# A convolution with mixed weight sets: the first images' operands in two row parts, weight points on TensorE, and statistics two tiles later

## The chip, the cores and the metric

The kernel runs on one core of one Trainium2 chip. The metric is the device time of one execution in microseconds. Every time below comes from the measured runs or from one profiled execution of the kernel before.

## The reference

`x` is 8 images of 64 channels and 48 x 48 pixels, float32. The reference normalizes each image over pairs of channels (32 groups), computes 8 logits for each pixel with a 1 x 1 convolution and takes their softmax, convolves the normalized image with 8 sets of 3 x 3 kernels to 64 channels each, adds a bias, and adds to `x` the sum of the 8 results weighted by the softmax:

```python
sel = jax.nn.softmax(conv1x1(gn(x), coupler_w) + coupler_b, axis=1)
sel = sel / sel.sum(axis=1, keepdims=True)
conv = conv3x3(gn(x), w).reshape(8, 8, 64, 48, 48) + bias
out = x + jnp.einsum('bschw,bshw->bchw', conv, sel)
```

## The kernel before

**Work and tiles.** Two images (64 channels each, so 128 partitions) make a round; there are four rounds. An image is 48 rows of 24 pairs of pixels, 1152 pairs, which are nine tiles of 128 pairs; a round has 18 tiles, nine of each image. A tile's results, two pixels by 512 columns (8 sets by 64 channels), lie in a `pair` of PSUM banks; three pairs are used in turn.

**The convolution.** Along a row it is computed from four "points": combinations of neighbouring pixels (`v_pts`, points 0 to 3), multiplied by matching combinations of the three kernel columns: point 0 half the sum of all three, point 1 the same with the middle one subtracted, points 2 and 3 an outer column itself. Each number is split in two float16 parts, a head and a tail. ScalarE makes the heads of `x` (`v_head`) and of the weights (`w_head`); tails (`v_tail`, `w_tail`) are the scaled value less the head, made by VectorE in the start and, for `x` in the rounds, by GpSimd (`input_tails`). SyncE's queue copies heads and tails into the operand layouts `op` and `op_two` (`fill_ops`, four transfers for each image and group of two points); a matmul takes 128 x 128 of them as weights and streams 512 columns of `w_head` or `w_tail`. `first_points` (points 0 and 1, nine matmuls) and `last_points` (points 2 and 3, ten) make 19 matmuls a tile.

**Order in a round.** TensorE's program does the last points of tile i, then the first points of tile i+2. ScalarE copies the first result, VectorE adds and subtracts (`seed`), so that the last points can be added on. Then VectorE multiplies the tile by the softmax weights (`multiply`: L640, L641), adds halves (`halve`: L649), and GpSimd adds quarters, what is left and the input (`finish`), with `input_and_bias` for three tiles at a time ahead of tiles 0 to 5. The pair of banks of tile i is free for tile i+3 when its half is done; the softmax weights of the next round are copied to `sel_now` at the round's end.

Between the tiles stand, in every engine's program by tile number, the steps of the next round: statistics (VectorE, tiles 0 and 1; aggregated at 2), `group_sums` (TensorE, 3), `group_variance` (VectorE, 4), `inverse_deviation` (GpSimd, 4), `scale_and_shift` (VectorE, 5), points (GpSimd, `POINTS_AT`), scaled points and heads (ScalarE, `HEADS_AT`, edges at `EDGES_AT`), tails (GpSimd, `TAILS_TILE`), `logits` (TensorE, 10), and the softmax (VectorE, 11 to 16).

**The start.** `x` comes in three loads, then the matrices for the group sums and six pieces of the weights (`w_low`, `w_high`: the two partition halves for each kernel row r). ScalarE takes the largest weight of each of three rows (`bound_of`, L506); VectorE and a tiny matmul turn it to a scale (`scales`), which every weight head needs. VectorE makes the weight sums and points (`kernel_sum`, `kernel_point1`, `kernel_point2`), point 0 and 3 of `x`, and all tails of `x` over the full 1152 pairs; GpSimd makes point 1 in three pieces and point 2 whole. TensorE does eight warm-up matmuls (L404), the logits of round 0, and waits for the operands:

```python
pe.wait_ge(ops_in[0][0], 16 * F_PARTS)
for a in range(2):
    for i in range(2):
        first_point(i, a, 0, i == 0)
first_points(2, 0)
```

## Time and profile before

| | us |
|---|---|
| median of 3 runs (352.16 to 352.71) | 352.54 |
| the profiled execution | 352.28 |
| its span, first to last instruction | 350.2 |
| TensorE busy | 314.3 |
| VectorE busy | 288.2 |
| GpSimd busy | 221.5 |
| ScalarE busy | 93.4 |

The engines overlap, so busy times don't add up. The page also shows the span in 40 slices, the transfers and the chain of waits that ended last.

### The profile page before, as it was taken

To read this page: it belongs to the slowest core of one execution; us is meant where nothing else is said; L and a number is where in the kernel's file an instruction comes from. 1 tells how busy PE (TensorE), PEld (TensorE's weight loads), DVE (VectorE), ACT (ScalarE), POOL (GpSimd) and SP (SyncE) were. 2 spreads that over 40 slices of the span, in tenths; PEclk is the share of its full clock that TensorE was granted. 3 is DMA by queue.
4 is the path that set the end of the run, shared out by engine and by line. 5 is a ranking of instruction groups with operands and counts; after the bars stand their busy time and mean duration, and the time that the engine had idled before them with its cause. 6 is when DMAs were issued, how large, how long until landed. Compare 5 with 4: busy or idle time off the path is not lost.

```text
span 350.2 us, 5352 instructions
## 1 busy us (share of the span) xinstructions
PE 314.3 (90%) x1612; PEld 142.9 (41%) x1612; DVE 288.2 (82%) x502; ACT 93.4 (27%) x127; POOL 221.5 (63%) x320
## 2 busy tenths in 40 slices
PE   0166779999999999999999999999999999999993
PEld 0142224444544434444544434445444344444441
DVE  2799999878799789877789699877789697777776
ACT  1665301162611201172521111173411111111110
POOL 3300068999793558999783568999774489533343
PEclk9996989999999999999999999999999999999998
DMA  6979996003984099005793198006770297002002
GB/s 194 212 147 195 306 198 139 4 0 97 214 195 116 6 254 219 5 0 154 155 239 70 47 240 196 0 0 176 160 147 1 79 236 172 0 3 66 0 0 67
DMA packets 28350, 41.24 MB, mean 118 GB/s; under 512 B 1968, under 2 KB 20528, under 8 KB 27952
## 3 DMA queue, kind: packets, MB, share of 16 engines
q1 hardware_dynamic: 27456, 37.49, 46.9%
q10 hardware_dynamic: 880, 3.58, 3.3%
q8 instruction: 6, 0.10, 0.1%
q14 instruction: 8, 0.07, 0.1%
HBM read 11.97 MB, written 4.72 MB: 48 GB/s over the span
## 4 chain that ended last, share of the span: by engine, by line
PE 66%; DVE 23%; issue 6%; DMA 2%; DVEq 1%; POOL 0%; SPq 0%; POOLq 0%
PE pair L342 41%; PE pair L354 14%; PE pair L350 10%; DVE high L641 4%; DVE pair L640 3%; DVE pair L624 3%; DVE pair L626 3%; DMA x_raw<-x 2%; DVE half L649 2%; DVE stats L544 1%; PE side L332 1%; DVE v_tail L800 1%; DVE w_tail L755 1%; DVE mix L609 1%; DVE w_sum L807 1%
## 5 line engine op out<-in xcount | busy, mean ns | idle before, releaser
L342 PE MATMUL pair<-w_head,op 128*128 128x512 f16 x864 | 236.4, 383 | 10.7 <-DVE half L649 5.5
L342 PEld LDWEIGHTS pair<-w_head,op 128*128 128x128 f16 x864 | 83.4, 99 | 116.6 <-DVE half L649 11.1
L354 PE MATMUL pair<-w_tail,op 128*128 128x512 f16 x288 | 109.9, 382 | 0.7 <-DVE w_tail L773 0.7
L479 ACT ACTIVATE m_sb<-pair 128x512 f32<-128x512 f32 x72 | 42.9, 597 | 225.9 <-PE pair L354 220.4
L937 POOL TENSOR_TENSOR quarter<-half 128x256 f32<-128x256 f32 x71 | 52.7, 743 | 72.4 <-DVE half L649 72.2
L640 DVE TENSOR_TENSOR pair<-pair,sel_now 128x512 f32<-128x512 f32 x71 | 49.5, 698 | 39.9 <-PE pair L354 39.4
L649 DVE TENSOR_TENSOR half<-pair,high 128x512 f32<-128x512 f32 x71 | 49.1, 692 | 9.9 <-DVE high L641 0.5
L350 PE MATMUL pair<-w_tail,op_two 128*128 128x512 f16 x144 | 54.6, 379 | 0.4 <-DVE w_tail L770 0.4
L624 DVE TENSOR_TENSOR pair<-pair,m_sb 128x512 f32<-128x512 f32 x72 | 49.6, 689 | 0.2
L626 DVE TENSOR_TENSOR pair<-m_sb,pair 128x512 f32<-128x512 f32 x72 | 49.3, 685 | 0.0
L641 DVE TENSOR_TENSOR high<-pair,sel_now 128x512 f32<-128x512 f32 x71 | 48.4, 681 | 0.0
L354 PEld LDWEIGHTS pair<-w_tail,op 128*128 128x128 f16 x288 | 28.3, 98 | 35.2 <-DVE w_tail L773 1.0
L925 POOL TENSOR_TENSOR bias_part<-bias_all,sel_now 128x384 f32<-128x384 f32 x24 | 19.9, 831 | 30.7 <-DVE sel_now L615 30.7
L941 POOL TENSOR_TENSOR mixed<-quarter 128x128 f32<-128x128 f32 x71 | 32.7, 461 | 5.6
L947 POOL TENSOR_TENSOR y_out<-mixed,x_res 128x128 f32<-128x128 f32 x71 | 32.4, 456 | 5.8 <-POOL mixed L941 0.5
L903 POOL TENSOR_TENSOR v_tail<-v_pts,v_head 128x576 f16<-128x576 f32 x24 | 30.2, 1281 | 0.0
L350 PE MATMUL pair<-w_tail,op 128*128 128x512 f16 x72 | 28.0, 389 | 0.5 <-DVE w_tail L755 0.5
L930 POOL TENSOR_TENSOR x_res<-x_res,bias_part 128x384 f32<-128x384 f32 x24 | 23.9, 997 | 2.3
L911 POOL TENSOR_TENSOR v_pts<-x_raw 128x1152 f32<-128x1152 f32 (+1 forms) x12 | 25.0, 2080 | 0.0
L350 PEld LDWEIGHTS pair<-w_tail,op_two 128*128 128x128 f16 x144 | 14.1, 98 | 17.7 <-DVE w_tail L770 0.9
L544 DVE BATCH_NORM_STATS2 stats<-x_raw 128x6 f32<-128x384 f32 x24 | 11.9, 548 | 5.9 <-DMA x_raw<-x 5.9
L450 ACT ACTIVATE v_head<-v_pts 128x1152 f16<-128x1152 f32 x12 | 14.0, 1165 | 0.7 <-ACT v_pts L441 0.4
(94 smaller groups left out, 148.2 us busy)
## 6 DMA issues: line engine op xcount, KB each, us to landing
op<-v_head SPq DMA_DIRECT2D x16, 600.0 KB, 7.8
op_two<-v_head SPq DMA_DIRECT2D x16, 300.0 KB, 9.0
op<-v_tail SPq DMA_DIRECT2D x16, 300.0 KB, 7.6
op<-v_head SPq DMA_DIRECT2D x16, 288.0 KB, 8.0
x_res<-x_pix SPq DMA_DIRECT2D x8, 576.0 KB, 6.9
out<-y_out SPq DMA_DIRECT2D x7, 576.0 KB, 3.9
x_raw<-x ACTq DMA_DIRECT2D x3, 1152.0 KB, 12.1
w_raw<-weight SPq DMA_DIRECT2D x6, 384.0 KB, 11.2
```

What stands on the lines that cost most here:

```text
L342: nc.tensor.matmul(dst, op[b][:, 0, j, at + r * PW:at + r * PW + P], w_head[:, j, r, :], start=fresh and r == 0, stop=False, skip_group_ch ...
L350: nc.tensor.matmul(dst, op[b][:, 0, j, after] if j == 0 else op_two[b][:, j - 2, after], w_tail[:, j, 1, :], start=False, stop=False, skip ...
L354: return nc.tensor.matmul(dst, op[b][:, 1, j, at:at + P], w_tail[:, j, 0, :], start=False, stop=True, skip_group_check=True)
L479: act.activation(m1_sb[:, i % LOOK, :], pair[i % SETS_OF_BANKS][:, 0, :], ACT.Copy) \
L624: dve.tensor_tensor(plus, minus, m1, ALU.add).then_inc(seeded, 1)
L626: dve.tensor_tensor(minus, m1, minus, ALU.subtract).then_inc(seeded, 1)
L640: dve.tensor_tensor(sets_of(i, 0), sets_of(i, 0), weights_of(i, 0), ALU.mult).then_inc(low_done, 1)
L641: dve.tensor_tensor(high[:, :, :, :], sets_of(i, SETS // 2), weights_of(i, SETS // 2), ALU.mult) \
L649: dve.tensor_tensor(half[:, i % LOOK, :, :, :].rearrange("p a s c -> p a (s c)"), pair[i % SETS_OF_BANKS][:, :, 0:N // 2], high[:, :, :, : ...
L937: pool.tensor_tensor(quarter[:, :, :, :].rearrange("p a s c -> p a (s c)"), hf[:, :, 0:2, :].rearrange("p a s c -> p a (s c)"), hf[:, :, 2 ...
L941: pool.tensor_tensor(mixed[:, :, :], quarter[:, :, 0, :], quarter[:, :, 1, :], ALU.add).then_inc(mixed_done, 1)
L947: pool.tensor_tensor(y_out[b][:, t, :, :], mixed[:, :, :], x_res[b][:, t, :, :], ALU.add).then_inc(out_done, 1)
```

## The change

Four edits are made together.

1. **Operands in two row parts.** For the first image pair, heads, tails and transfers of the operands are made first for rows 0 to 23 (`FIRST_ROWS`) and then for the rest. `first_fill(g, part)` issues five transfers in place of `fill_ops`' four. Parts run in the order (group 0, part 0), (1, 0), (0, 1), the load of `x_res`, (1, 1). TensorE waits for part 0 ahead of tiles 0 to 3, and for part 1 ahead of tile 4. The logits stand behind the first points of tiles 0 and 1.
2. **Weight points on TensorE.** `kernel_point1` adds the three kernel columns with float32 matmuls in a PSUM bank for each row r (a doubled identity as weights); `kernel_point2` subtracts twice the middle one in the same bank, once the point 1 head and tail are made. ScalarE and VectorE read heads and tails from there. The warm-up is 28 float32 matmuls of 128 columns ahead of the group sums, in place of eight float16 ones of 512 columns ahead of the logits.
3. **Three `x` points on GpSimd in pieces.** Points 1, 2 and 3 are made by GpSimd by thirds of the image; the last thirds of points 2 and 3 wait for the first weight head. GpSimd also makes the second part of the tails of points 2 and 3 (`late_tails`), after the first selection.
4. **Statistics two tiles later.** The statistics stand at tiles 2 and 3, aggregate 4, group sums 5, variance 6, scale 7; points at 5 to 8, heads 10 to 13, edges 11, tails 9 to 12, logits 11, the softmax from 12 on (divide_again and selection stay at 16). Round 0 of TensorE and all rounds of ScalarE are written out rather than looped.

```diff
+FIRST_ROWS = 24
+FIRST_PAIRS = FIRST_ROWS * PW
+FIRST_TILES = 4
...
-WARM = 8
+WARM = 28
...
-POINTS_AT = (5, 6, 8, 9)
-HEADS_AT = (8, 9, 12, 13)
-TAILS_TILE = (7, 8, 11, 12)
-EDGES_AT = 10
+POINTS_AT = (5, 6, 7, 8)
+HEADS_AT = (10, 11, 12, 13)
+TAILS_TILE = (9, 10, 11, 12)
+EDGES_AT = 11
...
+        w_points = [pair[2][:, 0, :], pair[2][:, 1, :], pair[1][:, 1, :]]
...
+            def first_fill(g, part):
+                pts = slice(2 * g, 2 * g + 2)
+                heads_made, tails_made, landed, fifth = ((h_first, t_first, first_in[g], first_in[g]),
+                                                         (h_done, t_done, ops_in[0][g], rest_in[g]))[part]
+                cols = slice(0, PW + FIRST_PAIRS) if part == 0 else slice(PW + FIRST_PAIRS, PADDED)
+                width = cols.stop - cols.start
+                below = slice(0, FIRST_PAIRS) if part == 0 else slice(FIRST_PAIRS, PAIRS)
+                above = slice(below.start + PW, below.stop + PW)
+                heads = v_head[0:C, pts, :]
+                wait(heads_made, 2 * g + 2)
+                sp.dma_start(op[0][0:C, 0, pts, cols], heads[:, :, cols]).then_inc(landed, 16)
+                sp.dma_start(op[0][0:C, 1, pts, cols], heads[:, :, cols]).then_inc(fifth, 16)
+                sp.dma_start(op[0][C:P, 1, pts, below], heads[:, :, above]).then_inc(landed, 16)
+                if g == 0:
+                    sp.dma_start(op_two[0][C:P, :, cols], v_head[0:C, 1, cols].unsqueeze(1).to_broadcast([C, 2, width])) \
+                        .then_inc(landed, 16)
+                else:
+                    sp.dma_start(op_two[0][0:C, :, cols], heads[:, :, cols]).then_inc(landed, 16)
+                wait(tails_made, 2 * g + 2)
+                sp.dma_start(op[0][C:P, 0, pts, cols], v_tail[0:C, pts, cols]).then_inc(landed, 16)
...
-            fill_ops(0, 0, 0)
-            fill_ops(0, 1, 0)
+            first_fill(0, 0)
+            first_fill(1, 0)
+            first_fill(0, 1)
             load_res(0, 0)
+            first_fill(1, 1)
...
-                    if more and i == 3:
+                    if more and i == 5:
                         group_sums(n + 1)
-                    if more and i == 10:
+                    if more and i == 11:
                         logits(n + 1)
...
+            def kernel_point1(r):
+                pe.wait_ge(w_low[r], 16)
+                for kx in range(K):
+                    last = nc.tensor.matmul(w_points[r], both_halves, w_raw[0:C, r, kx, :], start=kx == 0, stop=kx == K - 1)
+                last.then_inc(w_point1, 1)
+            def kernel_point2(r):
+                pe.wait_ge(w_high[r], 16)
+                pe.wait_ge(w_heads[0], r + 1)
+                pe.wait_ge(w_tails, r + 1)
+                nc.tensor.matmul(w_points[r], minus_twice, w_raw[C:P, r, 1, :], start=False, stop=True,
+                                 skip_group_check=True).then_inc(w_point2, 1)
+            pe.wait_ge(ready, 1)
+            for k in range(WARM):
+                nc.tensor.matmul(w_bank[:, 0:P], ones[:, :], ones[:, :], start=True, stop=True)
             pe.wait_ge(mats_loaded, 16)
             group_sums(0)
-            pe.wait_ge(ready, 1)
+            kernel_point1(0)
+            kernel_point1(1)
             pe.wait_ge(bounds_set, 2)
             pe.wait_ge(w_chain, 2)
             nc.tensor.matmul(w_bank[:, 0:2], ones[:, :], tiny[:, :], start=True, stop=False)
             nc.tensor.matmul(w_bank[:, 0:2], ones[:, :], w_max[:, :], start=False, stop=True).then_inc(w_added, 1)
+            kernel_point1(2)
+            for r in range(K):
+                kernel_point2(r)
+            pe.wait_ge(first_in[0], 16 * (F_PARTS + 1))
+            for i in range(2):
+                first_point(i, 0, 0, i == 0)
+            pe.wait_ge(c_tails, 1)
             pe.wait_ge(h_done, 1)
-            pe.wait_ge(w_chain, 3)
-            for k in range(WARM):
-                nc.tensor.matmul(w_bank[:, :], v_head[:, 1, 0:P], v_head[:, 1, 0:N], start=True, stop=True)
-            pe.wait_ge(c_tails, 1)
+            pe.wait_ge(h_first, 2)
+            pe.wait_ge(t_first, 2)
             logits(0)
-            pe.wait_ge(ops_in[0][0], 16 * F_PARTS)
-            for a in range(2):
-                for i in range(2):
-                    first_point(i, a, 0, i == 0)
+            first_point(0, 1, 0, True)
+            pe.wait_ge(w_tails, 6)
+            first_point(1, 1, 0)
             first_points(2, 0)
-            with pe.Fori(0, ROUNDS - 1) as n:
+            round_(0, True, True)
...
+            first_heads(1, 0)
             bound_of(1)
-            first_heads(1)
             bound_of(2)
-            first_heads(0)
+            first_heads(0, 0)
             act.wait_ge(w_chain, W_STEPS)
-            w_heads_of(0, slice(0, 1))
-            first_heads(2)
-            w_heads_of(0, slice(1, 2))
-            first_heads(3)
-            w_heads_of(0, slice(2, 3))
-            w_heads_of(1)
+            for r in range(K):
+                w_heads_row(0, r)
+            first_heads(1, 1)
+            first_heads(0, 1)
+            first_heads(2, 0)
+            first_heads(3, 0)
+            for r in range(K):
+                w_heads_row(1, r)
+            for r in range(K):
+                act.wait_ge(w_high[r], 16)
             w_heads_of(2)
+            copy_m1(0, 0)
+            w_heads_of(3)
             act.wait_ge(w_tails, 6)
             act.activation(w_tail[C:P, 3, 1, :], w_tail[C:P, 2, 1, :], ACT.Copy, scale=-1.0).then_inc(w_minus, 1)
-            w_heads_of(3)
+            exponentials(0)
+            copy_m1(1, 0)
+            first_heads(2, 1)
+            first_heads(3, 1)
             load_ahead(1)
...
-                    if more and i == 0:
+                    if more and i == 2:
                         dve.wait_ge(x_ahead, (n + 1) * 16)
                         statistics(range(CHUNKS // 2))
-                    if more and i == 1:
+                    if more and i == 3:
                         statistics(range(CHUNKS // 2, CHUNKS))
-                    if more and i == 2:
+                    if more and i == 4:
                         aggregate(n + 1)
-                    if more and i == 4:
+                    if more and i == 6:
                         group_variance(n + 1)
-                    if more and i == 5:
+                    if more and i == 7:
                         scale_and_shift(n + 1)
-                    if more and i == 11:
+                    if more and i == 12:
                         with_bias(n + 1)
                         maximum(n + 1)
-                    if more and i == 12:
+                    if more and i == 13:
                         less_maximum(n + 1)
-                    if more and i == 13:
+                    if more and i == 14:
...
             scale_and_shift(0)
-            first_input_point()
-            fourth_input_point()
-            input_tails_of(1, 1)
+            first_input_point(0)
+            input_tails_of(1, 0, 1)
+            first_input_point(1)
             weight_bound()
-            kernel_sum(0)
-            kernel_point1(0)
             scales()
-            input_tails_of(0, 2)
+            input_tails_of(0, 0, 2)
             coupler_parts()
-            kernel_sum(1)
-            kernel_point1(1)
-            input_tails_of(2, 3)
-            kernel_sum(2)
-            kernel_point1(2)
-            kernel_point2()
             first_point_tails()
-            input_tails_of(3, 4)
+            input_tails_of(1, 1, 1)
+            input_tails_of(0, 1, 2)
+            input_tails_of(2, 0, 3)
+            input_tails_of(3, 0, 4)
             second_point_tails()
...
-            for j in range(LOADS):
+            for j in range(LOADS - 1):
                 pool.wait_ge(x_loaded[j], 16)
-                raw_point(1, j)
+                for k in range(1, NP):
+                    raw_point(k, j)
+            pool.wait_ge(x_loaded[LOADS - 1], 16)
+            raw_point(1, LOADS - 1)
             inverse_deviation(0)
-            v_out, left, right = point_operands(2)
-            pool.tensor_tensor(v_out, left, right, ALU.subtract).then_inc(v_first[2], 1)
+            pool.wait_ge(w_heads[0], 1)
+            for k in range(2, NP):
+                raw_point(k, LOADS - 1)
+            def late_tails(k):
+                pool.wait_ge(h_done, k + 1)
+                pool.wait_ge(t_done, k)
+                cols = slice(PW + FIRST_PAIRS, PW + PAIRS)
+                pool.tensor_tensor(v_pts[:, k, FIRST_PAIRS:PAIRS], v_pts[:, k, FIRST_PAIRS:PAIRS],
+                                   norm_scale[:, 0:1].to_broadcast([P, PAIRS - FIRST_PAIRS]), ALU.mult).then_inc(late_scaled, 1)
+                pool.wait_ge(late_scaled, k - 1)
+                pool.tensor_tensor(v_tail[:, k, cols], v_pts[:, k, FIRST_PAIRS:PAIRS], v_head[:, k, cols],
+                                   ALU.subtract).then_inc(t_done, 1)
+            pool.wait_ge(sel_copied, 1)
+            for k in range(2, NP):
+                late_tails(k)
```

## Rows read from the trace of the kernel before

**Rows 1.** The page's first part: busy time of each engine, its share and instructions.

```profile
PE 314.3 (90%) x1612; PEld 142.9 (41%) x1612; DVE 288.2 (82%) x502; ACT 93.4 (27%) x127; POOL 221.5 (63%) x320
```

**Rows 2.** The chain of waits: start, duration in us, what.

```profile
88.79 1.34 PE side L332 x54
...
122.66 0.65 PE pair L342 x3
```

**Rows 3.** Timeline of TensorE: start, duration, operation, idle time before.

```profile
28.75 1.46 PE L342 MATMUL pair<-w_head,op 128*128 128x512 f16 x3 [3.47 <-DMA op<-v_tail]
...
47.77 1.46 PE L342 MATMUL pair<-w_head,op 128*128 128x512 f16 x3 [2.52 <-DVE half L649]
...
119.46 0.82 PE L342 MATMUL pair<-w_head,op 128*128 128x512 f16 x3 [0.62 <-DVE half L649]
...
137.09 0.28 PE L320 MATMUL side<-mean_var,mats 128*128 128x2 f32 x2
...
166.16 0.20 PE L332 MATMUL side<-cw_pts,v_head 128*128 128x32 f16 x2
```

**Rows 4.** Timeline of VectorE.

```profile
13.05 1.83 DVE L568 SCALAR_TENSOR_TENSOR shift<-group,norm_scale 128x1 f32<-128x1 f32 x1
...
20.06 0.15 DVE L828 TENSOR_SCALAR magnitude<-w_bank 128x2 int32<-128x2 int32 x1
...
22.72 0.69 DVE L807 TENSOR_TENSOR w_sum<-w_raw 128x512 f32<-128x512 f32 x1
...
28.38 2.31 DVE L755 SCALAR_TENSOR_TENSOR w_tail<-w_pts,half_scale,w_head 64x512 f16<-64x512 f32 x3
...
34.15 0.52 DVE L574 SCALAR_TENSOR_TENSOR logit<-side,undo,cb_all 128x288 f32<-128x288 f32 x1
...
45.60 0.70 DVE L640 TENSOR_TENSOR pair<-pair,sel_now 128x512 f32<-128x512 f32 x1 [0.25 <-DVE sel_now L615]
...
125.81 1.47 DVE L544 BATCH_NORM_STATS2 stats<-x_raw 128x6 f32<-128x384 f32 x3
...
160.31 0.70 DVE L640 TENSOR_TENSOR pair<-pair,sel_now 128x512 f32<-128x512 f32 x1 [0.79 <-PE pair L354]
...
161.74 0.69 DVE L649 TENSOR_TENSOR half<-pair,high 128x512 f32<-128x512 f32 x1
```

**Rows 5.** Windows: length, each engine's busy time, granted clock, DMA share, GB/s.

```profile
28.75:34.00 5.25, 4.71 (x11) 1.47 (x12) 5.15 (x7) 2.79 (x2) 0.00 (x0) 0.50 0.93 185
```

**Rows 6.** Timeline of ScalarE.

```profile
11.75 1.48 ACT L506 ACTIVATE w_pts<-w_raw 64x1536 f32<-64x1536 f32 x1 [6.75 <-DMA w_raw<-weight]
...
20.79 0.72 ACT L498 ACTIVATE w_head<-w_pts,half_scale 128x512 f16<-128x512 f32 x1 [1.82 <-DVE scale L835]
...
157.37 0.60 ACT L479 ACTIVATE m_sb<-pair 128x512 f32<-128x512 f32 x1 [0.66 <-PE pair L354]
```

**Rows 7.** Timeline of SyncE's queue, first operands.

```profile
19.05 0.68 SPq L252 DMA_DIRECT2D op<-v_head  x1
```

**Rows 8.** Timeline of GpSimd.

```profile
12.80 2.07 POOL L982 TENSOR_TENSOR v_pts<-x_raw 128x1104 f32<-128x1104 f32 x1
45.52 0.83 POOL L925 TENSOR_TENSOR bias_part<-bias_all,sel_now 128x384 f32<-128x384 f32 x1 [30.66 <-DVE sel_now L615]
46.43 0.99 POOL L930 TENSOR_TENSOR x_res<-x_res,bias_part 128x384 f32<-128x384 f32 x1
...
154.30 0.73 POOL L937 TENSOR_TENSOR quarter<-half 128x256 f32<-128x256 f32 x1
...
156.06 2.52 POOL L903 TENSOR_TENSOR v_tail<-v_pts,v_head 128x576 f16<-128x576 f32 x2
158.53 0.73 POOL L937 TENSOR_TENSOR quarter<-half 128x256 f32<-128x256 f32 x1
```

**Rows 9.** Groups of instructions, 6 to 45 us: busy, mean ns; idle before.

```profile
L404 PEld LDWEIGHTS w_bank<-v_head 128*128 128x128 f16 x8 | 1.0, 136 | 2.1 <-issue 2.1
...
L320 PEld LDWEIGHTS side<-mean_var,mats 128*128 128x128 f32 x2 | 0.5, 310 | 10.6 <-DMA mats<-matrices 10.6
```

More of the change, by code:

```diff
@@ L187, in program @@
         t_done = sem("t_done")
+        h_first = sem("h_first")
+        t_first = sem("t_first")
+        late_scaled = sem("late_scaled")
+        first_in = [sem(f"first_in{g}") for g in range(2)]
+        rest_in = [sem(f"rest_in{g}") for g in range(2)]
         logit_done = sem("logit_done")
@@ L324, in logits @@
             def logits(m):
+                pe.wait_ge(h_done, m * NP + 2)
                 pe.wait_ge(t_done, m * NP + 2)
@@ L339, in point @@
                 for r in range(K):
-                    if first and (j == 0 or r == 0):
+                    if first and (j < 2 or r == 0):
                         pe.wait_ge(w_heads[j], r + 1)
@@ L473, in load_ahead, with copy_m1, round_ @@
                 act.dma_start(x_raw[:, :], x_pair[m, :, :]).then_inc(x_ahead, 16)
[L475 removed]
+            def copy_m1(i, n):
+                act.wait_ge(m1_done, n * TILES + i + 1)
+                act.wait_ge(seeded, n * 2 * TILES + 2 * i + 2)
+                act.activation(m1_sb[:, i % LOOK, :], pair[i % SETS_OF_BANKS][:, 0, :], ACT.Copy).then_inc(m1_copied, 1)
+            def round_(n, more, ahead, copied=0):
                 for i in range(TILES):
[L477 to L480 removed]
+                    if i >= copied:
+                        copy_m1(i, n)
                     if more and i == EDGES_AT:
@@ L953, in round_ @@
                         finish(i, n)
-                    if more and i == 4:
+                    if more and i == 6:
                         inverse_deviation(n + 1)
@@ L1001 @@
     eye = np.eye(P, dtype=np.float32)
-    matrices = np.stack([0.5 * same_group, eye - 0.5 * same_group], axis=1)
+    matrices = np.stack([0.5 * same_group, eye - 0.5 * same_group, np.tile(eye[:C, :C], (2, 2)) * np.repeat([1, -2], C)[:, None]],
+                        axis=1).astype(np.float32)
     host = {
```

132 lines of the change are left out of this document (64 added, 68 removed).

## The prediction

> **What bounds the kernel now.** I read the page first: TensorE is busy nine tenths of the span [rows 1], so outside the start only its idle time can be won. The chain of waits then shows that a tile in the middle costs TensorE nothing but its own matmuls: 0.65 us for three of 512 columns, 0.216 us each, and 19 of them make 4.10 us a tile [rows 2]. VectorE needs less than that per tile, except where extra work is put between two tiles. The reader is to see two kinds of lost time.
>
> The first is the start. TensorE gets its first tile at 28.75 us, released by a transfer [rows 3], and VectorE multiplies the first tile only at 45.60 [rows 4]. In between, VectorE is one nearly unbroken queue: from the magnitude at 20.06 to the logits' bias at 34.15, then 11.45 us of softmax, weight tails and seeds to 45.60 [rows 4]. The DMA engines are busy at 0.93, 185 GB/s, while TensorE runs at a granted clock of 0.50, 1.2 GHz, having stood idle before 28.75 [rows 5, 3]. Tile 3 waits for the first half at 47.77, and its three matmuls take 1.46 us, the low level again, after 2.52 us of idleness [rows 3].
>
> The second is the head of each later round. From 119.46, where tile 2 begins, to the group sums at 137.09 there are 17.63 us [rows 3] for four tiles' work, 16.40 us: 1.23 us of idleness, because two lots of three statistics, 1.47 us, stand between VectorE's first tiles [rows 4]. About 0.2 us of it lies ahead of tile 3 and doesn't depend on them. Round 0 has no such loss: TensorE starts it late and slow.
>
> **The start after the change.** I walk the three engines in their new program orders; halves are 576 of 1152 columns.
>
> ScalarE: the first weight bound begins at 11.75 when its transfer lands [rows 6]. The third matrix adds 64 KB ahead of it, 0.35 us at 185 GB/s: 12.1. Three bounds (1.5 us each) with one half head between (0.7, as the 512-column head at 20.79) end at 17.4, the second half head at 18.1. Before, the first transfer of operands was issued at 19.05 [rows 7].
>
> VectorE no longer waits 1.83 us for the shift [rows 4]; this first shift isn't computed, its only user being a later round's point. Its queue is empty at 17.5 when the last bound comes. The bound sum is two tiny matmuls; I allow 0.8 us, so 18.3. The scales lie between 20.06 and ScalarE's first scaled head at 20.79: 0.7, so 19.0. Then one half tail (0.7; a weight tail of 512 columns is 0.77, a third of 2.31 [rows 4]), the coupler's small parts (I allow 0.7), three first-point weight tails 2.3, four more half tails 2.8, and three second-point weight tails 2.3. The seven operations that made weight sums and points (22.72 is one, 0.69) are gone: 19.0 + 8.8 = 27.8.
>
> Into this falls GpSimd's piecewise work: two last pieces of about 0.8 us each are held until the first weight head, so they start near 19.8, just where the coupler parts run. At 13.05 a one-column operation of VectorE lasted 1.83 us and ended at 14.88, when GpSimd's 2.07 us point from 12.80 ended at 14.87 [rows 4, 8]. So an operation with both inputs in SBUF can be held by one of GpSimd. I charge between 0 and 1.7 us and take 1.0: the logits' bias can start at 28.8. The Trainium skill's GPSIMD Engine Reference, section Key points, says that GpSimd shares its SBUF interfaces with VectorE and collides with instructions of two SBUF inputs; by that rule the sum keeps this 1.0, and without it the start would be 27.8; the trace agrees.
>
> TensorE: the nine float32 matmuls of the first point and three of the second have no row. One float32 matmul appears as two records; its weight load takes 310 ns against 136 ns for float16, both at low clock [rows 9]. The low bound is two float16 passes, 0.43 us; the high one 2 x 310/136 = 4.6 float16 prices at the low clock (0.427), 1.95 us. I take four prices at 2.4 GHz, 0.86, because the warm-up keeps TensorE busy until shortly before (the low end is float16's own work, the high end is the low clock, and a load isn't a stream). The Trainium skill's FP8 and Floating Point Precision, section TensorE Precision Notes, says that true FP32 makes four passes; by it a matmul would take 0.86 us or, at the low clock, 1.7, and no row here shows it. Rows 0 and 1 of point 1 then take 12.1 to 17.3, within the wait for the bound; row 2 takes 18.3 to 20.9. ScalarE turns them into heads at 0.65 each until 21.5, does four half heads and two edges (I allow 0.4 each) until 25.1, and the second point's rows until 27.0, each ahead of its VectorE tail. The second point's matmuls need the tails of point 1 at about 23.3 to 24.1, plus 0.86: no wait.
>
> The 28 warm-up matmuls of 128 columns cost 0.21 us each at 2.4 GHz, 0.43 at 1.2, from about 1.5 us. At the low clock for as long as after 28.75 (it was still 0.50 up to 34.00 [rows 5]) they end near 10, just ahead of the group sums, whose weight load waited until about 10.6 [rows 9]. I charge nothing; all at the low clock they would end at 13.5 and cost 2.9.
>
> The operands: a first part is 762 KB instead of 1488. Before, from the issue at 19.05 to the first tile it took 9.7 us [rows 7, 3]. The smaller one is issued at 18.2; half of that time and something for five separate issues gives 6.4: 24.6. Two first points (10 matmuls, 2.2) and the logits (1.34) [rows 2] end at 28.2, so VectorE's queue at 28.8 is the last to arrive; I take 29.0. From there the same operations as before take 11.45: first multiply at 40.45 instead of 45.60. Gain 5.15. The weights' last heads, the m1 copies (now moved ahead) and the other group's first part (due at 31, wanted at 33) are in time. The 2.5 us wait ahead of tile 3 and its slow matmuls move along unchanged.
>
> **What the start gives back.** The late tails are new on GpSimd, which before was idle until the selection at 45.52 [rows 8]; they wait for it too, at 40.3: two multiplies of 1.2 and two subtractions of 1.26 (half of the tail pair at 156.06), 4.9 us, so 45.2. Behind them stand the bias pair (45.52 to 47.42, 1.9 [rows 8]) and tile 0's finish at 47.1, while half 0 is ready at 42.5 (2.1 us from the multiply at 160.31 to the end of the half at 162.43 [rows 4]). SP's last operand transfer waits for the same tails, and behind it the second image's operands; these are wanted by tile 9, 20 us later, and cost nothing. GpSimd then has per tile a finish of 1.76 (154.30 to 156.06) and a bias pair, 3.6; a point is 2.06, a tail pair 2.5 [rows 8]. Tiles 0 to 4: 65.0; 5: 68.8; 6 with the deviation's 0.5: 73.1; 7: 76.9; 8: 80.7; 9 and 10 with tails: 84.9 and 89.2. TensorE reached the logits at 88.79 [rows 2]; it now wants them a tile of 4.10 later and 5.15 earlier: 87.7. Loss 1.5 in round 0.
>
> **The rounds.** Statistics two tiles later find a VectorE that waits 0.79 us of every tile [rows 4]. I walk it from F, the start of tile 2's first points: half 0 comes at F+6.35, and without statistics half 1 at F+9.6, a microsecond before TensorE wants it (F+10.6). Half 2 is ready at 12.8 (wanted 14.7), its seed behind the statistics at 15.4 (wanted 16.6); half 3 at 17.4 (wanted 18.8), its seed behind the second lot at 20.0 (wanted 20.7). So only the 0.2 ahead of tile 3 stays. Gain 1.0 in rounds 1 and 2, 2.0 in all; the bounds are nothing and the full 1.23 a round.
>
> But tails 1 moves from tile 8 to tile 10 and logits only from 10 to 11. In round 1 half 9 ends at 162.43 [rows 4]; GpSimd: finish 9 to 164.26, tails 0 to 166.75, finish 10 to 168.5, tails 1 to 171.0. The head of point 1 isn't later: tile 10's copy is at 157.37 [rows 6], and ScalarE's scale, head, copy, edges, scale and head (2.7, then to 161.5 for the next copy, then 0.6 + 0.7 + 2.4) bring it to 165.2. TensorE reached the logits at 166.16 [rows 3] and wants them at 170.3. Loss 0.8 in rounds 1 and 2. The softmax on VectorE begins one tile later and ends in the same tile. The round ended with 0.62 us of TensorE waiting for tile 17's half [rows 3]; one tile's slack of 0.79 less can add between nothing and 0.79 to it. I take the middle, 0.37, three times: 1.1.
>
> **Sum.** 5.15 + 2.0 - 1.5 - 1.6 - 1.1 = 2.95 us. The profiled execution took 352.28 us, 2.1 more than its span of 350.2 and 0.26 below the median of 352.54. So 349.3 for the execution, 349.6 for a median.
>
> **The rivals.** Within 0.2%, 0.7 us, a measurement can't tell a change here.
>
> First rival, no wait at the logits: GpSimd's order has room that I don't see, and the two later rounds and round 0 lose nothing there. For it, GpSimd kept up with the halves in this trace where no tails stood; against, a finish and a tail pair, 4.24, are longer than a tile. That is 3.1 us more gained: 346.5.
>
> Second, the operands land no sooner: they are rows of 1200 bytes and five issues, and if the count of pieces rather than the bytes sets their time, the first tile starts again 9.5 us after its issue, at 27.7 and the logits end 31.4; the bias follows at once. Gain 2.8 instead of 5.15: 352.0, no difference. A microsecond of slower issue more gives 353.0. For it, ten issues stand where eight did; against, the DMA engines are 0.93 busy, with bytes, in this stretch [rows 5]. I put it at 352.4.
>
> Third, on the other side: the float32 matmuls. Everything scales with their price d. Rows 0 and 1 must be through before the bound sum, and row 2 follows, nine in one line. At 1.2 us rows 0 and 1 end at 19.3, the bound sum at 20.1 and row 2 at 23.7, the chain is 2.8 us late, and nothing is left of the gain; at 1.7, the low clock throughout, the first bias comes at about 35.8, 6.8 late: 356.4, slower. The decisive point is 1.2 us. Against it, the clock came back under steady matmuls after 28.75 in this trace [rows 3, 5]: the matmuls of the middle run at 0.216.
>
> **How the numbers follow.** Forecast 0.60 (its own range 348.2 to 351.5, by a hold of 0 to 1.7, operands 1.5 us late, and waits at the logits from half to one and a half); no logits wait 0.14; operands no sooner 0.15; slow float32 matmuls 0.11. The range 347.2 to 352.8 takes in the second rival and part of the first, and leaves out about 0.18. Faster by over 0.2%: 0.60 + 0.14 = 0.74 and 0.01 from the partial cases of the others; same 0.14; slower 0.11.
>
> **What would show it.** Right: first tile near 24.6 at full clock, first bias near 29, first multiply near 40.5, waits of TensorE for v_tail ahead of the logits in three rounds (about 1.5, 0.8, 0.8), no idleness after tile 2 in rounds 1 and 2. Wrong: warm-up or w_points matmuls in front of the group or bound sums, w_points longer than 1.2 us each, first operands after 27, or VectorE held long beside GpSimd's pieces.

## The result and the profile after

The changed kernel takes 358.88 us, the median of 4 runs (358.80 to 359.66); the kernel before takes 352.62 beside it (352.16 to 352.71). The ratio is 1.0191, 95% interval 1.0178 to 1.0204: slower by 1.9%, outside the range and on the other side of no change. The profiled executions are 357.1 and 350.2 us long in their spans, 6.9 apart.

The page's first part, and the chain of waits from 10 to 40 us (start, duration, what):

```profile
PE 336.3 (94%) x1684; PEld 156.9 (44%) x1684; DVE 280.1 (78%) x496; ACT 93.7 (26%) x133; POOL 228.8 (64%) x329
```

```profile
2.61 9.92 DMA w_raw<-weight
12.53 0.04 issue
12.57 10.34 PE pair L435 x12
22.91 0.52 PE w_bank L455 x2
23.43 0.43 PE w_bank L456 x2
23.86 4.56 PE pair L435 x5
28.42 0.75 PE pair L443
29.16 0.11 PE pair L435
29.27 4.16 PE pair L443 x5
33.43 1.40 PE pair L374 x3
...
37.36 1.35 PE side L364 x54
38.72 0.03 issue
38.74 0.53 DVE logit L653
```

Behind the first weights' transfer, VectorE and DMA no longer stand in the chain of the start: from the landing at 12.57 to the logits' bias at 38.74 it is TensorE alone, whose busy time rose by 22.0 us over [rows 1]. A float32 matmul leaves two records, so twelve records of L435 are six matmuls and 10.34 us is 1.72 us for each; all twelve matmuls with the bound sum in their middle take from 12.57 to 33.4. The windows (columns as in [rows 5]) show the granted clock:

```profile
12.00:14.00 2.00, 1.43 (x2) 0.63 (x3) 1.25 (x5) 1.45 (x2) 0.55 (x1) 0.72 1.02 218
14.00:16.00 2.00, 2.00 (x4) 0.78 (x3) 1.21 (x3) 2.00 (x4) 0.00 (x0) 0.50 1.02 218
...
34.00:36.00 2.00, 2.00 (x6) 0.71 (x5) 1.97 (x4) 2.00 (x4) 0.00 (x0) 0.50 0.52 113
36.00:38.00 2.00, 2.00 (x37) 1.22 (x36) 0.51 (x1) 2.00 (x3) 0.00 (x0) 0.81 0.89 195
```

TensorE is busy in every window from 14 to 36, and the clock stays at 0.50, 1.2 GHz. It comes back only near 36.7, after 3.4 us of float16 matmuls. VectorE's timeline shows what it waits for:

```profile
17.96 0.15 DVE L887 TENSOR_REDUCE w_max<-w_max_part 64x1 f32<-64x3 f32 x1 [1.58 <-ACT w_junk L574]
23.89 0.16 DVE L892 TENSOR_SCALAR magnitude<-w_bank 128x2 int32<-128x2 int32 x1 [5.79 <-PE w_bank L456]
...
38.74 0.52 DVE L653 SCALAR_TENSOR_TENSOR logit<-side,undo,cb_all 128x288 f32<-128x288 f32 x1 [2.23 <-PE side L364]
...
50.12 0.70 DVE L719 TENSOR_TENSOR pair<-pair,sel_now 128x512 f32<-128x512 f32 x1 [0.25 <-DVE sel_now L694]
...
81.33 0.15 DVE L641 TENSOR_SCALAR norm_scale<-rstd 128x1 f32<-128x1 f32 x1 [1.75 <-POOL rstd L953]
81.52 1.77 DVE L647 SCALAR_TENSOR_TENSOR shift<-group,norm_scale 128x1 f32<-128x1 f32 x1
```

The bound is ready at 17.96, but its two tiny matmuls stand behind rows 0 and 1 on TensorE, 4.8 us. The first multiply, 45.60 before [rows 4], is at 50.12: 4.52 later. From there on TensorE's timeline, tile 3, then the waits of round 0, and the logits of round 1:

```profile
52.29 0.82 PE L374 MATMUL pair<-w_head,op 128*128 128x512 f16 x3 [2.53 <-DVE half L728]
...
84.05 0.81 PE L374 MATMUL pair<-w_head,op 128*128 128x512 f16 x3 [0.57 <-DVE pair L703]
...
86.57 0.82 PE L374 MATMUL pair<-w_head,op 128*128 128x512 f16 x3 [0.20 <-DVE half L728]
...
99.39 0.20 PE L364 MATMUL side<-cw_pts,v_head 128*128 128x32 f16 x2 [2.51 <-POOL v_tail L964]
...
126.27 0.82 PE L374 MATMUL pair<-w_head,op 128*128 128x512 f16 x3 [0.76 <-DVE half L728]
...
176.97 0.20 PE L364 MATMUL side<-cw_pts,v_head 128*128 128x32 f16 x2 [0.73 <-POOL v_tail L964]
```

I call the time from tile 3's first matmul to the next round's tile 2 the rest of round 0. It was 71.69 us, 47.77 to 119.46 [rows 3], and is 73.98, 52.29 to 126.27: TensorE is idle for 4.05 us of it and was for 0.62, and it is busy for 1.14 less, because before the clock was low at tile 3:

```profile
48.00:50.00 2.00, 2.00 (x6) 0.70 (x5) 2.00 (x5) 0.00 (x0) 1.75 (x4) 0.50 1.09 215
```

Rounds 1 and 2 take 77.58 each, before 77.53 and 77.54; the last one 75.67 in both. So 4.52 + 2.29 + 0.1 = 6.9: the start and the rest of round 0 hold the whole loss.

### The profile page after: what moved, and what is told of

It is laid out like the page before. It is cut to its first block, busy times and chain, and to the rows that moved or that the text cites. A ratio compares the mean times of both kernels' runs of the same rounds, so it can differ in the third digit from the quotient of the medians.

```text
span 357.1 us, 5439 instructions
## 1 busy us (share of the span) xinstructions
PE 336.3 (94%) x1684; PEld 156.9 (44%) x1684; DVE 280.1 (78%) x496; ACT 93.7 (26%) x133; POOL 228.8 (64%) x329
## 4 chain that ended last, share of the span: by engine, by line
PE 57%; DVE 16%; POOL 16%; issue 6%; DMA 3%; DVEq 1%; POOLq 0%; SPq 0%
PE pair L374 31%; PE pair L386 10%; PE pair L382 8%; POOL v_tail L964 4%; PE pair L435 4%; DVE high L720 3%; POOL quarter L998 3%; DVE pair L719 3%; DMA w_raw<-weight 3%; POOL v_pts L972 2%; DVE pair L703 2%; POOL mixed L1002 2%; DVE pair L705 2%; DVE half L728 2%; PE side L364 2%
## 5 line engine op out<-in xcount | busy, mean ns | idle before, releaser
L728 DVE TENSOR_TENSOR half<-pair,high 128x512 f32<-128x512 f32 x71 | 49.1, 692 | 9.8 <-DVE high L720 0.5
L977 POOL TENSOR_TENSOR v_pts<-x_raw 128x368 f32<-128x368 f32 (+1 forms) x9 | 7.0, 813 | 17.1 <-ACT w_head L567 12.5
L1054 POOL TENSOR_TENSOR v_pts<-v_pts,norm_scale 128x576 f32<-128x576 f32 x2 | 2.3, 1146 | 23.1 <-DVE sel_now L694 23.0
```

Of the source, the lines that this page charges most:

```text
L728: dve.tensor_tensor(half[:, i % LOOK, :, :, :].rearrange("p a s c -> p a (s c)"), pair[i % SETS_OF_BANKS][:, :, 0:N // 2], high[:, :, :, : ...
```

## The experiments

My theory of the start after this look: the twelve float32 matmuls are a line of 20.6 us on TensorE because they run at the low clock throughout, and they do so since they fill only 64 of 128 rows. The rivals: the clock hangs on the columns or the length of a matmul, or on the stage; or the line's place does the harm, ahead of the bound sum, and not its length. For round 0 it is GpSimd's late tails against the new order of the statistics. Unless it says otherwise, an experiment is the changed kernel with one edit. The price of a float32 matmul below is that of its two records together.

The clock blurs every comparison of round 0. In each trace but the changed kernel's it falls once or twice more after 42 us, to 0.50 for some three microseconds: near tile 3, and near the logits. Where TensorE has work then, this costs 1.2 to 1.6 us (the table at the end of this section gives its busy and idle time in the rest of round 0); where it would have waited anyway, nothing. At the logits it fell in six of the seven traces where TensorE had waited about 1.9 us or more for the tails, and in none of the six with a wait under 0.9. The changed kernel's trace is the seventh: it waited 2.51 us there and 2.53 ahead of tile 3, and the clock didn't fall. What decides on the fall near tile 3 no experiment here shows.

**Weight points on VectorE again**, the rest of the change left.

```diff
-            kernel_point1(0)
-            kernel_point1(1)
...
-            kernel_point1(2)
-            for r in range(K):
-                kernel_point2(r)
...
+                dve.tensor_tensor(w_sum[:, r, :], w_raw[:, r, 0, :], w_raw[:, r, 2, :], ALU.add).then_inc(w_sums, 1)
...
+                dve.tensor_tensor(w_pts[:, 0, r, :], w_sum[:, r, :], w_raw[:, r, 1, :], ALU.add).then_inc(w_point1, 1)
...
+                dve.tensor_tensor(w_pts[:, 1, :, :], w_sum[:, :, :], w_raw[:, :, 1, :], ALU.subtract).then_inc(w_point2, 1)
```

> The changed kernel with both weight points made by VectorE in SBUF again, everything else as changed. Theory A (the twelve float32 matmuls in one line on TensorE, 20.6 us of them, are what made the start late): the logits' bias on VectorE moves from 38.7 us to between 34 and 36, the first multiply from 50.1 to between 45.5 and 47.5, and the time falls from 358.9 by 3 to 4.5 us, to 354.4 to 356. What is left over 352.6 is then round 0, which lost about 4 us to GpSimd's late tails (2.3 net of the clock it kept). Rival (the row parts, their ten issues and the held pieces made the start late): the bias stays near 38 and the time within 1 us of 358.9.

354.97 us, ratio 1.0086 (1.0054 to 1.0119). TensorE's timeline of it:

```profile
18.12 0.56 PE L439 MATMUL w_bank<-tiny,ones 128*128 128x2 f32 x2 [6.60 <-DVE w_max L882]
...
24.31 1.03 PE L375 MATMUL pair<-w_head,op 128*128 128x512 f16 x2 [5.19 <-DMA op<-v_tail]
...
29.02 0.61 PE L383 MATMUL pair<-w_tail,op 128*128 128x512 f16 x1 [2.53 <-DVE w_tail L814]
```

The half operands land as forecast: first tile at 24.31, 4.44 earlier than [rows 3]. But TensorE then waits for VectorE's tails, the bias comes at 34.02 and the first multiply at 45.39, 0.2 earlier than before. So the first part's early landing is worth 0.2 us by itself, and the points on TensorE cost 50.12 - 45.39 = 4.7 us in these two traces. (The same start in another trace, that of the change with the later order below, had its first multiply at 48.27, which makes it 2.9; the medians differ by 3.9.) The logits of round 0 still wait 2.02 us. Its rest takes 75.26, 1.3 more than in the changed kernel though TensorE is idle for 1.3 less, because the clock falls twice.

**The same matmuls over 128 rows.** Both halves of the partitions go in, with the matrix halved, so each matmul also waits for the upper half's load.

```diff
-                    last = nc.tensor.matmul(w_points[r], both_halves, w_raw[0:C, r, kx, :], ...)
+                    last = nc.tensor.matmul(w_points[r], both_halves, w_raw[:, r, kx, :], ...)
```

> The changed kernel with its twelve float32 point matmuls over all 128 rows instead of 64 (both partition halves hold the same weights, so halves of the matrices give the same sums); they now wait for the upper half's load too, near 17 us. Theory A1 (64-row matmuls leave the granted clock low however long they run; 128-row ones, like those of the warm-up, raise it): the clock comes back within about 4 us of their start, each then takes 0.86 us, the twelve take 11 to 13 us instead of 20.6, the first tile starts near 29 to 30 instead of 33.4, and the time falls by 3 to 4.5 us. Theory A2 (512 float32 columns take 1.72 us and the low clock whatever the rows): they still take 20.6 us, but start 4 us later, the first tile starts near 37.5, and the time rises by about 4 us to 363.

358.98 us, ratio 1.0201 (1.0167 to 1.0235). Its timeline of TensorE, and its windows:

```profile
18.40 7.97 PE L436 MATMUL pair<-w_raw,mats 128*128 128x512 f32 x12 [6.72 <-DMA w_raw<-weight]
...
26.57 2.82 PE L436 MATMUL pair<-w_raw,mats 128*128 128x512 f32 x6
```

```profile
20.00:22.00 2.00, 2.00 (x4) 0.73 (x3) 0.00 (x0) 0.00 (x0) 0.00 (x0) 0.50 0.81 183
22.00:24.00 2.00, 2.00 (x4) 0.82 (x3) 0.00 (x0) 0.00 (x0) 0.00 (x0) 0.60 0.61 133
24.00:26.00 2.00, 2.00 (x6) 0.95 (x5) 0.00 (x0) 0.00 (x0) 0.00 (x0) 1.00 0.00 0
```

The clock comes back near 23.6, some 5 us into the line, where 64 rows had not brought it back in 21; a matmul then takes 0.94 us. Little is gained, because the line starts 5.8 us later, at the upper half's load, and the bound sum still stands behind it: the first multiply is at 48.70, 1.4 earlier. The rest of round 0, with two falls of the clock, takes 75.36 and gives the 1.4 back, so the time is the same.

**Matmuls over 64 rows in pieces of 128 columns.** Point 1's nine become 36. The output is then not the reference's; only the times are read.

```diff
+                for q in range(4):
+                    cols = slice(q * P, (q + 1) * P)
-                    last = nc.tensor.matmul(w_points[r], both_halves, w_raw[0:C, r, kx, :], ...)
+                        last = nc.tensor.matmul(w_points[r][:, cols], both_halves, w_raw[0:C, r, kx, cols], ...)
```

> The changed kernel with the nine point 1 matmuls of 512 columns cut in 36 of 128 columns over the same 64 rows. If the rows decide the granted clock, nothing changes: clock 0.5 from about 13 to 36 us, 0.43 us a piece, the time within 1 us of 358.9. If the length of a matmul decides it (the warm-up's had 128 columns and kept the clock up), the clock stays at or returns to 1.0 while they run, a piece takes 0.21 to 0.25 us, the first tile starts near 27, and the time falls by 4 us or more.

360.7 us in one run.

```profile
12.72 10.61 PE L437 MATMUL pair<-w_raw,mats 64*128 64x128 f32 x48 [0.90 <-DMA w_raw<-weight]
```

The first 24 pieces take 10.61 us, 0.44 each, and the clock is at 0.50 until the window from 36. The rival of the columns falls. The first multiply is at 50.15, as in the changed kernel; the time is 1.8 us longer and not within 1 us, because the clock falls twice in the rest of round 0, which takes 75.64.

**The warm-up over 64 rows.**

```diff
-                nc.tensor.matmul(w_bank[:, 0:P], ones[:, :], ones[:, :], start=True, stop=True)
+                nc.tensor.matmul(w_bank[:, 0:P], ones[0:C, :], ones[0:C, :], start=True, stop=True)
```

> The change as it is, with the warm-up of 28 float32 matmuls over 64 rows instead of 128; nothing else. If the rows decide on the clock, it stays at 0.50 during the warm-up, which ends near 13.6 instead of 10.2; the group sums and all that follow on TensorE are some 2.5 late, and the time is near 361. If rows don't matter and the clock stayed low later for another reason (the time of the stage, or the transfers beside it), the warm-up reaches full clock near 6 and ends at 10.2 as before: 358.9.

362.76 us in one run, 3.9 more than the changed kernel where I had about 2: the first multiply comes 2.9 later, at 53.02, and the rest of round 0 takes 74.90, with one fall of the clock. The warm-up of the changed kernel and of this one:

```profile
1.54 8.66 PE L448 MATMUL w_bank<-ones 128*128 128x128 f32 x56 [1.54 <-POOL v_tail L1029]
```

```profile
1.55 12.31 PE L448 MATMUL w_bank<-ones 64*128 64x128 f32 x56 [1.55 <-POOL v_tail L1029]
```

28 matmuls at 0.44 us each, the low level's price to the end, with nothing changed but the rows. With 128 rows they get faster on the way (11 records in the window 2 to 4, 20 in that from 8 to 10). The granted clock's column reads 1.00 here in both, in this run's even up to 50 us, where each 64x512 matmul takes 1.77; I go by the durations. With this run and the one in pieces, the rows decide here, and neither the stage nor the length of one matmul.

**The bound sum first**, only row 0 ahead of it.

```diff
             kernel_point1(0)
-            kernel_point1(1)
...
             nc.tensor.matmul(w_bank[:, 0:2], ones[:, :], w_max[:, :], ...)
+            kernel_point1(1)
             kernel_point1(2)
```

> The changed kernel with the two small matmuls of the bound sum behind row 0 of point 1 instead of behind rows 0 and 1. Theory L (the length of the float32 line on TensorE, 12 x 1.72 us from 12.6 on, sets the start): scales come at about 19 instead of 24.5, but row 2's point still ends near 29, the second point near 33 and the first tile starts at 33.2 to 33.5; the time stays within 1 us of 358.9. Theory O (what hurt was that the bound sum stood behind two rows): the start gains most of the 5 us by which the scales come sooner, 354 to 355.

357.79 us, ratio 1.0151 (1.0135 to 1.0166). The bound sum is at 17.96 instead of 22.85, and of these 4.9 us only 2.0 reach the first multiply (48.13), since the first tile still stands behind the whole line, in which the second point now waits 1.49 us for a tail of VectorE (32.16). The rest of round 0 grows by 1.3, to 75.32: the clock falls at tile 3 and at the logits there. The order is worth 1.1 us of the time; that the line's length is the rest follows from the run with VectorE's points and wasn't tested apart.

**128 rows, loads row by row, bound sum first, 14 more warm-up matmuls**: all four remedies together.

```diff
+MORE_WARM = 14
...
-            for half_p, loaded in ((0, w_low), (1, w_high)):
-                for r in range(K):
+            for r in range(K):
+                for half_p, loaded in ((0, w_low), (1, w_high)):
```

> The changed kernel with the point matmuls over all 128 rows, the weight loads row by row (lower and upper half of row 0 first), 14 more warm-up matmuls behind the group sums, and the bound sum behind row 0. If 128-row float32 matmuls hold the clock up when it was up before: clock 1.0 from 5 us on, 0.94 us a matmul, points of row 0 from about 15, scales near 20.5, point 1 complete near 25.5, first tile near 29, the logits' bias between 31 and 33 instead of 38.7, and the time 352.5 to 354 (GpSimd's late tails and the schedule still cost their 3.5 to 4). If the clock falls all the same: 0.5 from about 17 on, and 356 to 359.

357.43 us, ratio 1.0146 (1.0118 to 1.0175).

```profile
14.35 2.74 PE L437 MATMUL pair<-w_raw,mats 128*128 128x512 f32 x6
20.68 0.35 PE L458 MATMUL w_bank<-tiny,ones 128*128 128x2 f32 x2 [3.59 <-DVE w_max L891]
```

The price is right, 2.74 us for the first three matmuls, 0.91 each. But in this order of loads the third bound comes 2.6 us later (20.39 against 17.83 with VectorE's points); TensorE is idle for 3.59 us until then and its clock falls again, and the first operand transfers are issued at 21.11 (18.68 in the changed kernel). The first multiply is at 46.86, 3.3 earlier, of which the rest of round 0, again with two falls, gives 1.3 back (75.28). Fast matmuls over 128 rows need the loads that the bound needs too.

**The kernel before with the new order of the rounds alone** (statistics at tiles 2 and 3, tails at 9 to 12, logits at 11).

```diff
-TAILS_TILE = (7, 8, 11, 12)
+TAILS_TILE = (9, 10, 11, 12)
```

> The kernel before with the statistics, points, heads, tails, logits and softmax steps moved as in the change, nothing else. Theory: in rounds 1 and 2 the gain at the head of the round (1.0 us) is taken back at the logits (0.7 of waiting for GpSimd's second tails, 0.15 slower logits) and at the round's end (0.15), so the round takes 77.5 to 77.6 us as before; round 0 has nothing to gain and loses 0.7 to 1.2 at the logits and the end. Together 353.2 to 353.9 us. Rival (the later schedule itself costs round 0 the 4 us that the changed kernel lost there): 356 to 357. If the logits' wait doesn't come without the late tails: 350.5.

353.61 us, ratio 1.0021 (1.0006 to 1.0036). The logits wait 0.74, 0.74 and 0.72 us in the three rounds, where the change waits 2.51 in the first. The order by itself costs 0.2%. In its trace rounds 1 and 2 take 77.59 and 77.57, as before, and the rest of round 0 72.66, 1.0 more: what the order gains at a round's head it loses at the logits, and round 0 has no loss at its head to win back.

**Late tails on VectorE**, with the points there too (to be read beside the first experiment).

```diff
+                    if late and i < 2:
+                        input_tails_of(2 + i, 1, 3 + i)
...
-            for k in range(2, NP):
-                late_tails(k)
```

> The kernel of the run with VectorE's weight points, with the late tails of x (rows 24 and up of points 2 and 3) made by VectorE behind tiles 0 and 1 of round 0 (two operations of 0.75 us) instead of by GpSimd (four operations, 4.9 us) ahead of its bias and finish steps. Theory: GpSimd then starts round 0 at 45 as in the kernel before and isn't behind at the logits; TensorE's wait there falls from 2.0 to 0.7 us and other waits of round 0 go; round 0 (tile 3 to the next round's tile 2) takes 72.3 to 73 instead of 75.3 us, and the time falls from 355.0 by 2.3 to 3 us to 352 to 352.7. Rival (GpSimd's late tails aren't the cause, the later schedule alone is): under 0.5 us gained.

352.78 us, ratio 1.0022 (1.0007 to 1.0036): 2.2 us less than with them on GpSimd. The wait at the logits falls from 2.02 to 0.84. Tile 3 waits 0.83 instead of 2.52 us, but GpSimd has no part in that:

```profile
44.13 1.49 PE L375 MATMUL pair<-w_head,op 128*128 128x512 f16 x3
...
47.30 0.82 PE L375 MATMUL pair<-w_head,op 128*128 128x512 f16 x3 [0.83 <-DVE half L709]
```

The clock fell at 43.4 in this trace, so TensorE took until 46.5 for work that it otherwise ends near 45, and was back at the high level when tile 3 came. It starts at 47.30, only 0.26 earlier. Of the 3.0 us by which the rest of round 0 is shorter in the traces (72.24), 0.6 is idle time and 2.4 the clock, which doesn't fall in it at all. The fall that is missing at the logits goes with the shorter wait there; the one at tile 3 isn't shown to have to do with the tails.

**The kernel before, statistics two tiles later, but tails and logits in time.** The first pair's tails stay at 7 and 8 and the logits at 10; the last points' steps go to 9 to 14.

```diff
-POINTS_AT = (5, 6, 8, 9)
-HEADS_AT = (8, 9, 12, 13)
-TAILS_TILE = (7, 8, 11, 12)
+POINTS_AT = (5, 6, 9, 10)
+HEADS_AT = (9, 10, 13, 14)
+TAILS_TILE = (7, 8, 12, 13)
```

> The kernel before with the statistics at tiles 2 and 3, group sums at 5, variance and deviation at 6 and scale at 7 as in the change, but GpSimd's points at 5, 6, 9 and 10 and tails at 7, 8, 12 and 13, heads at 9, 10, 13 and 14, logits and softmax where they were before (10, and 11 on). Theory: GpSimd has the second tails ready a tile before TensorE wants them, so no wait at the logits, and the end of the round waits 0.6 as before; rounds 1 and 2 take 76.4 to 76.7 us instead of 77.5, round 0 as before: 350.3 to 350.9. If the head of the round isn't gained by moving the statistics: 352.5. If the heads come too late for the copies (scale at tile 7, first head at tile 9): a wait of TensorE for a seed near tile 11 or 12 and 352 to 354.

348.82 us, ratio 0.9918 (0.9896 to 0.9939): faster than both kernels, and 1.5 better than I had expected. No wait at the logits is left, the head of each round has none, and a round takes 76.4 us instead of 77.5:

```profile
118.00 0.82 PE L343 MATMUL pair<-w_head,op 128*128 128x512 f16 x3 [0.51 <-DVE half L650]
...
194.43 0.82 PE L343 MATMUL pair<-w_head,op 128*128 128x512 f16 x3 [0.52 <-DVE half L650]
```

That is 2.2 us, 0.6%, and it is the order's. The spans differ by 3.6: the rest of round 0 takes 69.96 instead of 71.69, and 1.6 of this is the clock, which fell here at 43.7 and was high again at tile 3:

```profile
44.80 1.49 PE L343 MATMUL pair<-w_head,op 128*128 128x512 f16 x3
...
48.04 0.82 PE L343 MATMUL pair<-w_head,op 128*128 128x512 f16 x3 [0.90 <-DVE half L650]
```

The six runs lie in two groups, four at 348.6 to 348.9 and two at 350.3 and 350.6, where I had expected them. None of the 17 runs of the kernel before beside them is below 351.7. So the 0.8% is measured, but that the order brings about the part over 0.6% isn't shown.

**The change with this order.** The same three lines, the logits at 10 and the softmax from 11 on.

> The change as it is, but with the tails of a pair at tiles 7, 8, 12, 13, its points at 5, 6, 9, 10 and the logits at tile 10 again; the statistics stay two tiles later. If the loss of the later rounds and part of that of round 0 is the order behind the statistics, the two middle rounds take 76.4 instead of 77.6, round 0 some 2 us less than its 74.0, and the time is 354.2 to 355.2, still above the kernel before since the first stage is untouched (first multiply at 50.1). If GpSimd's late tails of the first pair are what holds round 0, that round gains under 0.7 and the time is 355.8 to 356.6.

352.52 us, ratio 1.0005 (0.9982 to 1.0028), from 12 runs that spread from 349.0 to 356.0. In the profiled one the rest of round 0 takes 71.64 us and the two rounds 76.44 each, 2.3 + 2.3 = 4.6 less than the change's. The clock falls once in this round 0, at 51.3, where the changed kernel's didn't; TensorE is idle for 0.51 us in it instead of 4.05. So GpSimd's late tails cost round 0 little once the next pair's tails are in time: in this trace it is idle again for 1.08 us ahead of them. The other 1.9 us lie in the start, where the clock fell 0.8 us later and rose near 34.2 instead of 36.7; how long the start takes varies with that, and I have no run that fixes it.

**Everything that helped**: row parts, points and late tails on VectorE, this order.

> The row parts with the weight points on VectorE and the late tails on VectorE, with the order of the rounds that took 76.4. If the two gains add, the first multiply is at 45.1 and tile 3 at 47.3, 0.7 before that of the kernel before with this order alone, round 0 takes 70.3 to 71, and the time is 348.2 to 349.2. If the late tails on VectorE cost round 0 what the start gained, it is 349 to 349.8, no better than the order alone (348.8).

348.67 us, ratio 0.9899 (0.9884 to 0.9914), the best, and not to be told from the order alone (348.82). Tile 3 starts at 47.24, 0.80 earlier, and the rest of round 0 takes 70.98, 1.0 more than there. The early start is given back.

The traces side by side, in us; "rest" is the rest of round 0, and "falls" counts how often the clock falls in it:

| | first multiply | rest | TensorE busy in it | idle | falls |
|---|---|---|---|---|---|
| the kernel before | 45.60 | 71.69 | 71.07 | 0.62 | 1 |
| the change | 50.12 | 73.98 | 69.93 | 4.05 | 0 |
| points on VectorE | 45.39 | 75.26 | 72.47 | 2.79 | 2 |
| 128 rows | 48.70 | 75.36 | 72.68 | 2.68 | 2 |
| bound sum first | 48.13 | 75.32 | 72.65 | 2.67 | 2 |
| 128 rows, row by row | 46.86 | 75.28 | 72.52 | 2.76 | 2 |
| before, new order | 45.98 | 72.66 | 71.16 | 1.50 | 1 |
| late tails on VectorE | 45.13 | 72.24 | 70.08 | 2.16 | 0 |
| before, tails in time | 45.87 | 69.96 | 69.44 | 0.52 | 0 |
| the change, tails in time | 48.27 | 71.64 | 71.13 | 0.51 | 1 |
| everything that helped | 45.07 | 70.98 | 69.92 | 1.06 | 0 |

## Why the prediction was wrong

**The step that failed** is "I take four prices at 2.4 GHz, 0.86, because the warm-up keeps TensorE busy until shortly before". The matmuls took 1.72 us, the price that the third rival gave for the low clock. The two prices were in the text, and the choice between them went by the argument that a busy TensorE has its clock. [Rows 3, 5] showed the clock's return under matmuls of 128 rows only, and the new ones have 64. At 0.11 this rival was given too little: no row spoke for a 64-row matmul at the high level. The prediction's own sign of being wrong, `w_points` longer than 1.2 us each, is what the trace shows. The Trainium skill, TensorE: Matmul & The Clock Gate, section What's actually happening, says that the throttled state is the default and activity releases it; here TensorE was busy from 14 to 36 us at 0.50, so that sentence alone doesn't foretell this kernel's clock. For the price itself the four passes that the prediction cites from the Trainium skill fit: 1.72 us at the low level, 0.94 at the high one in the run with 128 rows.

**The rival's own sum was short.** It put the first bias at 35.8; it came at 38.74. It let the bound sum and row 2 be late, but not what is behind row 2 on TensorE: three matmuls of point 2, 5.2 us, and then two first points, most of them at the low clock, 3.8 instead of 2.2 (33.36 to 37.20). Its 356.4 was 2.5 us below the result.

**Had TensorE made the points at no cost**, the rest of the start would have held. In the run with VectorE's points the bias is at 34.02, and the five operations between 22.33 and 26.65 are 4.3 us of it: 29.7 without them, where I had 29.0. That is worked out, not run. From the bias to the first multiply it took 11.38 us (predicted 11.45). The hold beside GpSimd's pieces was near 1.2 (taken as 1.0): two coupler operations of VectorE lasted 0.87 and 0.74 in the changed kernel, and 0.23 and 0.25 in the kernel before. The operands landed at 24.3 (24.6). (The 762 KB of a first part are counted in thousands and the 1488 in units of 1024; the part is 744 of the same units, just half, and the sum doesn't change.)

**Round 0.** The late tails took 5.1 us (4.9), and GpSimd's tails 1 ended 49.1 us after the first multiply (48.8). The wait at the logits was 2.51 and not 1.5: TensorE reached them 46.8 us after the first multiply, where I had 47.3, and GpSimd was 0.3 later. What I hadn't priced is the deviation. `inverse_deviation` stands in the same late queue of GpSimd, so VectorE waited 1.75 us for it and its one-column shift was then held 1.77 us; TensorE lost 0.77. The logits themselves took 0.16 more and the round's end 0.14. Together with some 1.3 us that the high clock after tile 3 saved here, this is the 2.29. That saving isn't shown to be the change's: in the six other traces with GpSimd's late tails and this order the clock fell, and the rest of round 0 took 74.9 to 75.6.

**Rounds 1 and 2** went as written. No idle time is left at their head (gain 1.0), the logits wait 0.73 and 0.72 (predicted 0.8), the round's end 0.76 instead of 0.62, and the logits themselves take 1.50 instead of 1.34: +0.05 each where I had +0.17. The end's 0.37 was 0.14, and nothing in the last round.

**What the forecast of the gain missed** is that both good ideas were tied to a bad one each. Statistics two tiles later gained 1.1 us in each of two rounds with tails and logits in time, and nothing with these moved behind them, where they cost 0.2% by round 0. The half operands bring the first tile 4.4 us forward, and 0.2 of it gets through, because the tails of VectorE end the start.

## What to carry to other kernels

Don't price a matmul at the full clock because TensorE is busy around it: look in the trace for matmuls with as many rows at that clock, and where there are none, let both prices decide the chances. Work put on an idle engine is in program order with what the critical chain sends through it; list what stands behind it to the last user, at the worse price. When one step is moved later, move only what depends on its slack: here the same move of the statistics gained 1.1 us a round or nothing, by whether the tails and logits went along. And before a difference of a microsecond or two is put down to an edit, look whether the granted clock fell in the same places in both traces.

## What the runs showed that was not expected

Unbroken float32 matmuls over 64 rows ran at 1.2 GHz for 21 us, at 128 columns as at 512 (0.44 and 1.72 us each), and 28 of 64 x 128 as a warm-up never got faster. Over 128 rows the same matmuls took 0.91 to 0.94 us once the clock was back. Whether float16 matmuls over 64 rows would do the same wasn't tried. When VectorE took over the late tails, GpSimd's quarter beside one lasted 1.23 us, and 0.73 elsewhere. The later falls of the clock moved from trace to trace of the same or nearly the same program, and with them up to 3 us of TensorE's busy time in round 0.
